# Vision tower with two expert layers on one core: patch weights in two loads, block loads released by VectorE, second pieces requested six blocks ahead

## What is computed

```python
h = _L0_tok_ref(x, W, b, class_token, pos_embed)    # einsum('bpi,hi->bph') + b, times positions
h = h + _L0_attn_ref(_layernorm(h), Wk, bk, Wq, bq, Wv, bv)
h = h + _L0_ffn_ref(_layernorm(h), expert_sel, keys, values)     # top 2 of 32, hidden 128, relu
h = h + _L1_attn_ref(_layernorm(h), k)                           # decayed sums, times |delta|
h = h + _L1_ffn_ref(_layernorm(h), router_w, router_b, w1, b1, w2, b2)   # top 2 of 16, hidden 512
```

## Time and profile before

| | us |
|---|---|
| median of 3 runs (range) | 1286.27 (1285.39 to 1287.85) |
| the profiled execution, its whole time | 1299.48 |
| its span, first to last instruction | 1297.8 |

### The profile page before, as it was taken

How to read it: one execution, slowest core, us unless ns; L and a number is a source line. 1 busy time by engine, 2 the same in 40 slices (tenths; PEclk the granted TensorE clock), 3 DMA queues, 4 the chain that set the end, 5 groups by cost and what they waited for, 6 DMA issues and landing times.

```text
span 1297.8 us, 22134 instructions
## 1 busy us (share of the span) xinstructions
PE 1004.7 (77%) x6263; PEld 848.0 (65%) x6263; DVE 875.6 (67%) x3298; ACT 512.7 (40%) x1345; POOL 703.5 (54%) x653
## 2 busy tenths in 40 slices
PE   6999999999999536666674666366624999999995
PEld 3566776767676525555674665256524999999995
DVE  1487888888888635455665665476643777788785
ACT  1254535544553211111332333254421555565552
POOL 1036657776775455656546566555563455555554
PEclk8998999999999657766876667576656999999998
DMA  9655566566630325557775553244244767899883
GB/s 373 268 204 178 177 239 206 206 216 221 222 126 19 108 76 164 170 161 220 241 211 172 145 154 104 73 154 159 78 139 141 248 219 245 266 323 307 289 290 131
DMA packets 121049, 247.96 MB, mean 191 GB/s; under 512 B 21787, under 2 KB 88555, under 8 KB 114656
## 3 DMA queue, kind: packets, MB, share of 16 engines
q1 hardware_dynamic: 76224, 190.74, 44.1%
q0 software_dynamic: 19584, 34.70, 8.0%
q10 hardware_dynamic: 25120, 21.12, 5.4%
HBM read 203.03 MB, written 47.46 MB: 193 GB/s over the span
## 4 chain that ended last, share of the span: by engine, by line
PE 40%; DVE 25%; issue 14%; another core or an unknown queue 8%; DMA 5%; ACT 3%; SPq 3%; ACTq 2%; DVEq 0%; POOL 0%; POOLq 0%
PE ps L882 9%; PE ps L864 6%; PE ps L685 4%; PE ps L682 3%; DMA xin<-lists_L 3%; PE ps L746 2%; PE ps L730 2%; DVE xin L1743 2%; PE ps L845 2%; DVE xin L1724 2%; SPq L532 2%; PE ps L678 2%; PE ps L703 1%; DVE ntok L1382 1%
## 5 line engine op out<-in xcount | busy, mean ns | idle before, releaser
L1969 POOL DMA_INDIRECT results_L<-xin x322 | 318.4, 989 | 278.0 <-DVE xin L1743 164.7
L1942 POOL DMA_INDIRECT lists_L<-rows,slots x250 | 280.2, 1121 | 191.8 <-issue 172.7
L685 PE MATMUL ps<-xin,w_emb 128*128 128x512 f32 x280 | 133.7, 614 | 10.0 <-DMA w_emb<-in_w_main 10.0
L882 PE MATMUL ps<-xin,QK 128*128 128x128 f32 x804 | 115.4, 294 | 29.1 <-DVE xin L1743 13.7
L882 PEld LDWEIGHTS ps<-xin,QK 128*128 128x128 f32 x804 | 106.3, 208 | 32.7 <-issue 26.3
L882 PE MATMUL ps<-xin,UH 128*128 128x128 f32 x800 | 114.0, 293 | 13.0 <-DVE xin L1743 9.6
L845 PE MATMUL ps<-ident,xin 128*128 128x128 f32 x322 | 76.0, 326 | 53.7 <-DMA xin<-lists_L 33.5
L882 PEld LDWEIGHTS ps<-xin,UH 128*128 128x128 f32 x800 | 105.9, 208 | 15.4 <-issue 14.4
L1065 ACT ACTIVATE h0T<-ps 128x256 f32<-128x256 f32 x81 | 30.8, 383 | 205.0 <-remote 75.6
L864 PE MATMUL ps<-x_hi,x_lo 128*128 128x256 f32 x320 | 99.1, 310 | 9.9 <-DVE x_lo L1718 7.5
L1951 POOL TENSOR_TENSOR x_lo<-xin,x_hi 128x2048 fp32r<-128x2048 f32 x13 | 60.1, 4625 | 76.6 <-ACT x_hi L1046 76.3
(11 more groups left out here) (275 smaller groups left out, 2420.3 us busy)
## 6 DMA issues: line engine op xcount, KB each, us to landing
xin<-in_x_main SPq DMA_DIRECT2D x48, 1536.0 KB, 7.1
xin<-in_w_L SPq DMA_DIRECT2D x80, 578.0 KB
xin<-in_w_L SPq DMA_DIRECT2D x89, 128.0 KB
xin<-lists_L SPq DMA_DIRECT2D x80, 132.0 KB
xin<-in_w_L ACTq DMA_DIRECT2D x73, 128.0 KB
xin<-in_difference SPq DMA_DIRECT2D x13, 640.0 KB
xin<-in_distance SPq DMA_DIRECT2D x13, 640.0 KB
x_hi<-results_L SPq DMA_DIRECT2D x11, 640.0 KB
```

Source lines behind the costliest of these rows:

```text
L685: mm = pe.matmul(psE[h], w_emb[:, k, :], xin[h][c][:, n, :], start=(k == 0), stop=False, skip_group_check=True)
L882: mm = pe.matmul(o, hTb[p2][:, f, q * 128:(q + 1) * 128], w2[:, f * D:(f + 1) * D], start=(f == 0), stop=(f == l.FC - 1))
L1942: pool.indirect_dma_start(out=lists[l.name], out_offset=bass.IndirectOffsetOnAxis(ap=slots_of(l, g, h)[:, t, k:k + 1], axis=0), in_=buf[:, ...
L1969: pool.indirect_dma_start(out=results[l.name], out_offset=bass.IndirectOffsetOnAxis(ap=xblk[u][:, q, PLACE:PLACE + 1].bitcast(U32), axis=0 ...
```

## The change

1. **Patch weights in two loads.** ACT issues slices 0 to 5 (384 KB, `w_first_in`), then slices 6 to 17 (768 KB, `w_emb_in`), then `w_rest`. TensorE waits for the first before chunk 0, and for the rest before chunk 1.
2. **Group 0 plain.** Chunk 2 of group 0 is multiplied as plain float32. The rounding on ACT and DVE for group 0 is gone, and that of group 1 no longer waits for TensorE.
3. **First layer's loads wait for `y_ready`.** DVE copies the two addresses of each partition to `place` in every block, behind its wait for `y_out`, which now stands ahead of its wait for TensorE. POOL reads its addresses there.
4. **`AHEAD` = 6.** ACT's load of block s + 6 stands in step s; of its 12 padding writes 8 stand in step 0 and 4 in step 1, and `dispatched` in step 2 (before: step 4).
5. **SP's mixing loads.** `load_rows` moves from offset 4 to 6, behind `load_difference`, with waits of its own for the scatters.

```diff
-            if i >= l.unroll or l is L1:
+            if l is L1:
                 eng.wait_ge(k.y_out[u], k.y0[u] + 16 * l.Q * j)
+            elif i >= l.unroll:
+                eng.wait_ge(k.y_ready, i - l.unroll + 1)
...
-        AHEAD = 4
+        AHEAD = 6
...
+            def landed(l, enough):
+                for b in range(max(0, enough - NB), enough):
+                    sp.wait_ge(K[l.name].y_out[b % NB], K[l.name].y0[b % NB] + 16 * l.Q * (b // NB + 1))
...
-                yield 4, load_rows, g + 3
                 if g + 2 >= 0:
                     yield 5, load_difference, g + 2
+                yield 6, rows_landed, g + 3
+                if g + 2 >= 0:
                     yield 7, load_distance, g + 2
...
+                        if g == 0 and c < 2:
+                            pe.wait_ge((w_first_in, w_emb_in)[c], 16 * (c + 1))
...
-                    elif c == SPLIT:
+                    elif c == SPLIT and g > 0:
...
-            act.dma_start(w_emb[:, :, :].rearrange("p k d -> p (k d)"), a["w_main"]).then_inc(w_emb_in, 16)
-            act.dma_start(w_rest[:, :], a["w_rest"]).then_inc(w_rest_in, 16)
+            for first, end, got in ((0, KC, w_first_in), (KC, KT, w_emb_in)):
+                act.dma_start(w_emb[:, first:end, :].rearrange("p k d -> p (k d)"), a["w_main"][:, first * D:end * D])                    .then_inc(got, 16)
+            act.dma_start(w_rest[:, :], a["w_rest"]).then_inc(w_emb_in, 16)
...
-            high(0, 0, 0)
...
-            low(0, 0, 0)
...
                     restore(u, j)
+                    dve.wait_ge(k.y_out[u], k.y0[u] + 16 * l.Q * j)
+                    if l is L0:
+                        dve.tensor_copy(place[:, u, :], xblk[u][:, :, PLACE].bitcast(U32))
                     dve.wait_ge(k.y_ps, k.i0 + i + 1)
-                    dve.wait_ge(k.y_out[u], k.y0[u] + 16 * l.Q * j)
...
+                        where = place[:, u, q:q + 1] if l is L0 else xblk[u][:, q, PLACE:PLACE + 1].bitcast(U32)
```

More of the change, by code:

```diff
@@ L341, in build @@
                 for u in range(NB)]
+        place = sb("place", [128, NB, 2], U32)
         xTb = [h0T[h][:, :, :].rearrange("p i t -> p (i t)")[:, 0:2 * 128] for h in range(2)]
@@ L406, in build @@
         ssq, mag = LNC.base[:, 1, :], LNC.power[:, 1, :]
-        w_emb_in = sem("w_emb_in")
-        w_rest_in = sem("w_rest_in")
+        w_first_in, w_emb_in = sem("w_first_in"), sem("w_emb_in")
         w_hi_ready = sem("w_hi_ready")
@@ L617, in mid_class, with rows_landed @@
                 return L0.class_of(done // (TILES * ROWS))
+            def landed(l, enough):
+                for b in range(max(0, enough - NB), enough):
+                    sp.wait_ge(K[l.name].y_out[b % NB], K[l.name].y0[b % NB] + 16 * l.Q * (b // NB + 1))
+            def rows_landed(g):
+                landed(L0, L0.enough(mid_class(g)))
+                load_rows(g)
             def early(g):
-                assert L0.enough(mid_class(g + 3)) <= EARLY[g] + 4 + 1 - NB or g < LAST and EARLY[g] + 4 >= L0.blocks
-                yield 4, load_rows, g + 3
                 if g + 2 >= 0:
                     yield 5, load_difference, g + 2
+                yield 6, rows_landed, g + 3
+                if g + 2 >= 0:
                     yield 7, load_distance, g + 2
@@ L631, in _ @@
             among.left()
-            waited = L0.blocks - NB
             for g in range(LAST + 3, MG):
                 if g > LAST + 3:
[L635 to L639, removed]
+                    rows_landed(g)
                 load_distance(g)
@@ L654, in load_left @@
             def load_left(g, u, j):
-                done = L1.enough(L1.class_of(g))
-                for b in range(max(0, L1.blocks - NB), done):
-                    sp.wait_ge(K["L1"].y_out[b % NB], K["L1"].y0[b % NB] + 16 * L1.Q * (b // NB + 1))
+                landed(L1, L1.enough(L1.class_of(g)))
                 load_end(g, u, j)
@@ L663, in _ @@
         def _(pe):
-            pe.wait_ge(w_emb_in, 16)
             def embed(g, h, j, first, end):
@@ L670, in embed @@
                     if n == 0:
+                        if g == 0 and c < 2:
+                            pe.wait_ge((w_first_in, w_emb_in)[c], 16 * (c + 1))
                         pe.wait_ge(chunk_in[h][c], (j + 1) * (32 if c == CHUNKS - 1 else 16))
-                        if c == SPLIT:
-                            pe.wait_ge(split, g + 2)
+                        if c == SPLIT and g > 0:
+                            pe.wait_ge(split, g + 1)
                         if c == 0 and g >= FIRST:
@@ L1035, in high @@
                 act.wait_ge(chunk_in[h][SPLIT], 32 * (j + 1))
-                if not (isinstance(g, int) and g == 0):
+                if g > 1:
                     act.wait_ge(chunk_used[1 - h][SPLIT], j + h)
@@ L1216, in load @@
                         load_part(act, l, i % U, i // U, 1)
-                    elif PADS[l.name] + 4 * (i - AHEAD) < l.E:
-                        pads(act, l, PADS[l.name] + 4 * (i - AHEAD), PADS[l.name] + 4 * (i - AHEAD) + 4)
+                    elif i == AHEAD:
+                        pads(act, l, PADS[l.name], l.E - 4)
+                    else:
+                        pads(act, l, l.E - 4, l.E)
                 works = [(xT, 2), (load, AHEAD)] if l is L0 else [(high, 2), (gelu, 1)]
@@ L1343, in low @@
             def low(g, h, j):
-                dve.wait_ge(x_hi_ready, g + 1)
+                dve.wait_ge(x_hi_ready, g)
                 x = xin[h][SPLIT][:, :, :].rearrange("p k n -> p (k n)")
@@ L1968, in send_results @@
                     for q in range(l.Q):
+                        where = place[:, u, q:q + 1] if l is L0 else xblk[u][:, q, PLACE:PLACE + 1].bitcast(U32)
                         pool.indirect_dma_start(
-                            out=results[l.name], out_offset=bass.IndirectOffsetOnAxis(
-                                ap=xblk[u][:, q, PLACE:PLACE + 1].bitcast(U32), axis=0),
+                            out=results[l.name], out_offset=bass.IndirectOffsetOnAxis(ap=where, axis=0),
                             in_=yblk[u][:, q, :], in_offset=None, bounds_check=last, oob_is_err=False)\
```

4 lines of the change are left out of this document (2 added, 2 removed).

## The result

| | before | after |
|---|---|---|
| median of 21 runs each (range) | 1289.49 us (1282.61 to 1295.36) | 1284.75 us (1270.55 to 1298.91) |
| ratio, 95% interval | | 0.9945 (0.9922 to 0.9969) |
| profiled execution, its span | 1299.48, 1297.8 us | 1270.55, 1268.8 us |

The change gains about 7 us, 0.55%, where 19 were forecast. (The two medians are only 4.7 us apart: seven of the 21 runs after the change fell in a slower state of the chip, and the ratio leaves such runs out.) The median lies 0.75 us above the stated range. The kernel before was itself 3 us slower over 21 runs than in the three shown at first. The profiled execution of after is the fastest of its 21, and that of before took longer than any of the 21 timed ones. So their 29 us of difference must not be read as the effect; I compare stage by stage and over several traces.

What follows compares the result with a forecast made beforehand. TensorE was taken to bound the front, DMA to run nearly full before 45 us, and waits between engines to bound the blocks. Blocks -12 and start -7 made -19, shifted from the profiled run to 1267 us; range 1248 to 1284.

Steps and rivals of the forecast that it cites:

- first rival: Blocks gain nothing, because unnamed stops set the pace or loads don't go out earlier; only the start's 7 us, 1279; chance 0.22.
- sign of being wrong: Wrong if the front doesn't end earlier, or the blocks' stretch changes by less than 5 or more than 20 us.
- The start, -7: Group 0: smaller first weight load starts matmuls 2.0 us earlier, plain chunk 2 saves 4.9; bounds -4.9 and -7.5.
- fourth rival: Start's gain lost again because images of groups 1 to 3 come late; only the blocks' -12, 1274; chance 0.08.
- Loads, -18: Blocks: loads released by y_ready shorten TensorE's 26.5 us of waits for loads; bounds 0 and -35.6.
- 15.9 us of them whole: TensorE's load waits from 488 to 608 us, counted as full gain because POOL lags there.
- POOL's floor: Two sends of 1.28 us, 2.57 us a block; forecast blocks at 2.78 stayed above, so POOL wouldn't give the gain back.
- the small part of the term: Of 10.6 us of load waits outside 488 to 608 us, a fifth counted as gain: 2 us.
- Padding, +2: First blocks: six ahead and all padding waited for earlier make ACT's copy about 2 us later, once; bounds 0 and +3.
- Copies, +4: Blocks: 81 DVE copies of the places take 13 to 25 us, a third of 13 counted; bounds 0 and +25.
- The sum: Whole kernel: blocks -18 + 4 + 2 = -12, start -7, together -19 us.

Runs made afterwards that it cites:

- the start alone: Kernel before with only parts 1 and 2 of the change (two weight loads, group 0 plain), three runs: ratios 0.9943, 0.9966 and 0.9978 to before.
- e4_ahead4: Changed kernel with AHEAD = 4 and the old padding, release by y_ready kept: ratio 0.9947 to the kernel before.
- e8_by_y_out: Changed kernel with first-layer loads waiting for y_out again, six ahead kept: ratio 1.0025 to the kernel before.
- i1_later_wait: Changed kernel with ACT's old padding, its padding wait behind the rows of blocks 5 and 6, then loads 8 to 10 together: ratio 0.9885 to before.
- e5_copies4: Changed kernel with three more copies of the places per block, into a spare buffer: ratio 1.0052 to the kernel before.
- h2_blocks_only: Kernel before with only parts 3 to 5 of the change, start as before: ratio 0.9986 to the kernel before.

## Why the prediction missed

Its first rival is what happened: only the start was left. Its own sign of being wrong came too: from the first scatter to block 80 the stretch went from 333.4 to 337.0 us, and 12 less were forecast.

1. **The start, -7.** Right in mechanism, 0.85 too large. The first matmul gained 1.7 of 2.0 us; from there to the last slice 18.60 us passed where 18.2 were worked out. At the first scatter 5.8 us of it arrived by the medians of the traces, with ratios of 0.9943 to 0.9978 for the start alone. The fourth rival falls. The 7.15 us for the rounded products were read from a trace whose 1.2 GHz stretch was longer than in the three others with that start; without that, about 5.2 us were there to gain at the last slice.
2. **Loads, -18.** This step failed, twice over. The waits for loads did go, all of them, but not by the release: with it and four ahead 27.0 us of them stay. And it failed to count 15.9 us of them whole because the blocks would still be above POOL's floor. On X, blocks 8 to 36 took 3.25 to 3.32 us in place of 3.20 and 3.24. The pace there is the sends' 2.57 us and POOL's gaps (19.9 us before, 21.4 after), and it is the same with the waits (`e4_ahead4`, 3.27) and without (`e8_by_y_out`, 3.17). The rows for this were there: idle time of 33.7 us for something unnamed and engines standing together with their inputs done, once in a period whose idle time behind eight sends did not vary. That pointed at a pace-setter that a load can't move. Against that, the small part of the term, 2 us from outside, was mis-sized: blocks 36 to 80 gained 5 us on X and 14 us on Y (means 184.8 and 170.8). The waits were shared out by where they were long, and the gain came from block 36 on, where on Y POOL's idle time for DVE could fall (30.1 to 10.7 us).
3. **Padding, +2.** Measured 4.9 us at ACT's copy, and out of the bound of 3. Before the change, ACT's copies at 497.00 were compared with the end of the wait at 499.47 alone. But two further things stand ahead of the copy now: the load's own issues (487.52 to 488.60, 1.1 us), and a wait that ends later as measured from the first scatter (12.7 us behind it, before 11.4). 2.5 + 1.1 + 1.3 = 4.9. `i1_later_wait` gave the 5 us back to block 36, and lost some 2 of them again from there to block 80.
4. **Copies, +4.** 81 of them take 199 ns each, 16.1 us of DVE, inside the bounds. In `e5_copies4` three more per block lengthened the block stretches by 0.9 us. Taken by the trace, one copy costs next to nothing; the timed runs speak for more, and this stays open.

POOL's sends took 987 ns on average beside the copies and 988 without them, and 989 beside four copies in each block. On Y they took 990 to 1004 ns with the copies and 985 and 995 without, far less than the 200 ns of a copy. So nothing of GpSimd being held by DVE shows here. By the rule of the Trainium skill ("DMA: Bandwidth & Descriptors", section "SWDGE vs HWDGE vs iDMA") that speaks of DVE's 2-port mode locking GpSimd out of the rings, the sends would have had to lengthen with the copies, if these run in that mode: no run here shows it, and none shows the mode.

5. **The sum.** On X the blocks' part is 0: by the traces of four kernels with it, +7 to block 36, of which 5 are the padding's, and -5 from there on; by the timed runs of `h2_blocks_only`, -2, within noise. So it is about -6 in all, against -19. On Y both parts gain; their product, 0.9955 x 0.9858 = 0.981, would be some 22 us, near the forecast, though the changed kernel as a whole was not run there. The range held neither a spread of chips nor the 3 us by which before's own median moved.

## What to carry to other kernels

A wait that goes is worth what its stretch's pace-setter lets through: look for the interval that repeats exactly (here eight sends and a gap), and ask first whether the edit touches what makes it. Waits that end together on several engines with no named releaser may belong to a pace-setter that no edit of the loads moves. Where a change has two edits for one wait, run each alone: here the one that carried the argument was not the one that removed the wait. If an engine's load is moved ahead of its other work, everything that the load waits for moves ahead of it too, and each of its issues counts.

## What the runs showed of the hardware

- The same kernel takes 1285 to 1289 us on three chips and 1174 to 1175 on two. The difference lies in stretches with dense indirect scatters, and in the mixing (160 to 172 us on the first kind and 120 to 127 on the second, in the kernels with all sends, from the start of the last first-layer scatter to the first of the second layer). The front is alike, and from there to the end it is 295 to 310 us against 290 to 292. On the first kind, POOL has a gap of 2.8 to 2.9 us behind most runs of eight sends, which the second kind doesn't have (19 to 24 us in all from block 8 to 36 against 1.1 at most), and TensorE, DVE and ACT stop together for up to 3 us in it.
- With half the scatters these blocks take 1.8 us each on both.
- A gap of 1.09 us of TensorE in a busy front was followed by some 10 us at the 1.2 GHz level in the profiled execution of before. Near 380 us all sixteen kernels with the new start have a gap of 1.05 to 1.09 us: six of them fell to the 1.2 GHz level behind it, for some 3 or 10 us, and ten, the changed kernel's profiled execution among them, stayed at the 2.4 GHz level.
